# Cross-attention with an image-prompt branch: the output projection in fp32r from high and low parts that Pool splits, and three slots of exponentials

## The chip, the cores and the metric

The kernel runs on one core of one Trainium2 chip. A core has TensorE (PE; its weight loads are listed as PEld), VectorE (DVE), ScalarE (ACT), GpSimd (POOL) and SyncE (SP), which run side by side and wait for one another through semaphores. The metric is the device time of one execution in microseconds (us); lower is better. Three runs of the kernel before gave a median of 502.31 us, from 501.15 to 502.61.

## The reference

Sixteen batches of 256 queries attend, in 20 heads of 16 channels, to 248 text keys with a plain softmax, and to 8 image keys (4 dummy ones and 4 masked by boxes) with a softmax of their own. The two results are added, projected by `w_out`, and the bias and the input are added. Cut to what matters, everything in fp32:

```python
q = split(x @ w_q);  k = split(text @ w_k);  v = split(text @ w_v)     # x (16,256,320), ctx (16,256,512)
out_text = softmax(q @ k.T / 4) @ v                                    # 20 heads, text = first 248 rows
k_ip, v_ip = split(ip @ w_k_ip), split(ip @ w_v_ip)                    # last 8 rows
out_ip = softmax(q @ k_ip.T / 4 + mask(bbox)) @ v_ip
out = (merge(out_text) + merge(out_ip)) @ w_out + b_out + x            # w_out (320,320)
```

## The kernel before, in words

**Numbers.** The projections of q, k and v are fp32r matmuls (one pass over the columns) of operands that are split in a high part (rounded to fp32r) and a low part (the rest): high times high, high times low, low times high. ACT makes high parts, DVE low ones. The values matmul (exponentials times v) and the output projection are plain fp32 matmuls; a plain fp32 matmul stands in the trace as two records.

**Stages.** Batches are made in groups of two. A group has 10 projection tiles (3 of k, 4 of v, 3 of q), numbered n = 10 g + j. The first 12 run alone at the start. The others are hosted, one at a time, in the attention of earlier batches: `batch(t)` attends batch t and hosts 5 tiles of a later group, for t = -1 to 11. The batches t = 12 to 15 host nothing, and `batch(16)` only ends batch 15. Projected q, k and v go to DRAM and come back, stacked anew, for each batch.

**One batch.** Each engine runs its own list, written out by hand: ten slots p = 0 to 9, one for each pair of heads. In slot p PE makes the transposed scores of pair p of batch t (`key_scores`, line 880), and the scores of pair p of batch t + 1 (`query_scores`, line 819), from which DVE takes row maxima (`maxima`, line 664). ACT exponentiates (line 576) into `probs`, four slots of 1024 columns. In even slots PE multiplies by v, four heads (a quad) at a time (`values`, line 895); odd slots host a tile. The tables at the end of the file say in which slot the rest stands. For each of the 5 quads: ACT copies the result from PSUM (`evacuate`, line 568), DVE transposes it in 32x32 blocks and takes reciprocals of the sums (`invert`, lines 715 and 718), POOL multiplies and adds the two branches into `o_norm_t` (lines 478 and 483). DVE turns that back, two quads a piece, as c = 0, 1, 2 (`turn_back`, line 723, slots 8, then 2 and 4 of the next batch), and PE projects (`project_out(b, tile of 128 queries, c)`, line 904): tile 0 in slots 3 (c = 0, 1) and 5 (c = 2), tile 1 in slot 9. DVE adds the residual (`finish`, line 733).

**POOL's list.** For each batch b, `normalise(b)` begins with the residual: it waits for the load of x of this batch (`xr_loaded`) and adds the bias (line 468); only then come the quads k = 0 to 4 of batch b. In k = 2 it also spreads the values of the next batch (line 457). POOL, like every engine, works its list strictly in order.

**SP's list.** SP issues nearly all transfers, in order. In `batch(t)` the load of the residual of batch t (line 338) stands behind the store of the last tile of the batch before, a load of context or x, the k stacks and values of later batches, and the store of an output.

**The start.** PE begins `batch(0)` with a wait on the semaphore `small`, which both the load of the output weights (line 302) and that of the bias (line 303) raise; SP issues them behind the row maxima of batch 0 (line 283). x of the second group is loaded between the k stores and the k loads of the first, and split by ACT (line 502) and DVE (lines 628 and 630) between the lone tiles.

Of the kernel before, what the change touches and what calls it, by code (L numbers as in the profile page):

```python
# [4 lines left out]
B, S, D, C = 16, 256, 320, 512  # L5
# [30 lines left out]
def xattn(nc, x, xT, ctxT, ctx_sp, bbox, wq, wk, wv, wk_ip, wv_ip, wo, bias, grid, kaux, vones, out):  # L36
# [12 lines left out]
    with ctx:  # L49
# [6 lines left out]
        probs = sb("probs", [P, 4, 4 * S])  # L56
        o_all = sb("o_all", [P, 2 * SLOTS * S + 3 * OC * S])
# [3 lines left out]
        x_all = sb("x_all", [P, 6 * S])  # L61
        out_sb = sb("out_sb", [P, OT, D])
        wo_sb = sb("wo_sb", [P, OC, D])
# [10 lines left out]
        v_stage = sb("v_stage", [P, 2, D])  # L74
# [6 lines left out]
        raw = sb("raw", [P, XC * GT])  # L81
        sp_ctx_hl = stack2[:, 0:2 * CC * P].rearrange("p (s c n) -> p s c n", s=2, c=CC)
# [7 lines left out]
        o_norm = o_all[:, at:at + 2 * OC * S].rearrange("p (u c n) -> p u c n", u=2, c=OC)  # L90
        o_norm_t = o_all[:, at + 2 * OC * S:at + 3 * OC * S].rearrange("p (c j n) -> p c j n", c=OC, n=32)
# [3 lines left out]
        def x_raw(g):  # L95
            cols = o_all[:, 0:XC * GT] if g < 2 else raw[:, :]
            return cols.rearrange("p (c n) -> p c n", c=XC)
        flat_p = probs[:, :, :].rearrange("p a n -> p (a n)")
        wkip_raw, wvip_raw, wk_raw = (
            flat_p[:, i * CC * D:(i + 1) * CC * D].rearrange("p (c n) -> p c n", c=CC) for i in range(3))  # L100
# [5 lines left out]
        first_q = [flat_p[:, at:at + 2 * GT].bitcast(f32r).rearrange("p (s n) -> p s n", s=2)  # L106
                   for at in (2 * CC * D + 2 * D - 128, 0, CC * D)]
        x_res = x_all[:, 0:2 * OT * D].rearrange("p (u t n) -> p u t n", u=2, t=OT)
        parts = x_all[0:B * NIP, :].rearrange("p (k n) -> p k n", k=6)
        grid_sb, inside, box_mask, dummy_mask = parts[:, 0:2, :], parts[:, 2, :], parts[:, 3, :], parts[0:B, 4, :]  # L110
        zeros = parts[0:B, 5, :]
# [36 lines left out]
        ld = {n: sem("loaded_" + n) for n in ("sp", "wkip", "wvip", "wq", "wk", "wv", "small", "boxes")}  # L148
# [34 lines left out]
        o_ready = sem("o_ready")  # L183
        out_ready, out_done, out_stored = sem("out_ready"), sem("out_done"), sem("out_stored")
# [27 lines left out]
        slot = lambda u, p: (PAIRS * u + p) % 4  # L212
# [20 lines left out]
        def _(sp):  # L233
# [112 lines left out]
            load_x(1)  # L346
# [4 lines left out]
            load_stack_q(0)  # L351
            lone(5, 7)
# [7 lines left out]
            def first_batch():  # L360
                for n in range(TILES, 19):
                    store_tile(n)
# [50 lines left out]
        def _(pool):  # L413
# [7 lines left out]
            pool.memset(o_norm_t[:, :, :, :], 0.0).then_inc(preset, 1)  # L421
            pool.wait_ge(ld["boxes"], 48)
            pool.wait_ge(preset, 4)
# [19 lines left out]
            for par in range(2):  # L443
                pool.memset(slots(par, 0)[1], 1.0).then_inc(preset, 1)
                pool.wait_ge(preset, 5 + 3 * par)
# [13 lines left out]
            def store_special(i):  # L459
# [4 lines left out]
                    .then_inc(ksp_stored, 16)  # L464
            def normalise(b):
# [4 lines left out]
                for k in range(QUADS):  # L470
# [4 lines left out]
                    if k == 2 and b + 1 < B:  # L475
# [6 lines left out]
                    half = (k % 2) * DH  # L482
                    pool.tensor_tensor(o_norm_t[:, k // 2, :, half:half + DH], out[:, 0:S // 32, :],  # L483
                                       out[:, S // 32:, :], ALU.add).then_inc(o_added, 1)
            spread_values(0)
            pool.wait_ge(ld["small"], 32)
            for b in range(B):
                normalise(b)
        @block.scalar
        def _(act):  # L490
# [53 lines left out]
            tile(3)  # L544
            split_x(1)
            for n in (4, 5):
                tile(n)
# [16 lines left out]
            def evacuate(b, k):  # L564
                n = QUADS * b + k
                act.wait_ge(pv_ready, n + 1)
                need(act, turned, n + 1 - SLOTS)
# [421 lines left out]
```

## Time and profile before

| | |
|---|---|
| median of 3 runs | 502.31 us (501.15 to 502.61) |
| the profiled execution, its own time | 503.35 us |
| its span, first to last instruction | 501.4 us |
| mean granted TensorE clock | 0.986 |
| PE busy | 463.9 us, 93% |
| DVE busy | 393.7 us, 79% |
| ACT busy | 277.1 us, 55% |
| POOL busy | 154.6 us, 31% |

Busy time is the time in which an engine had an instruction under way; matmuls overlap, so the start-to-start distance of two of them, not the duration of one, is what one costs. Idle time names the engine, or the transfer, whose semaphore ended it. The tenths by slice on the page show PE at 9 from slice 7 to slice 33 of 40, and the granted clock at 9 in all slices but the sixth and seventh, where it is 7.

### The profile page before, as it was taken

The page shows a single profiled execution, that of the slowest core. Times are in us where ns is not written, and L with a number is a line of the kernel's source. Part 1 is how long each engine was busy: PE and PEld are TensorE (multiplying, and loading weights), DVE is VectorE, ACT ScalarE, POOL GpSimd, SP SyncE. Part 2 cuts the span into 40 slices and gives each one's busy share as a digit, 9 for nine tenths or more (in the row PEclk, how much of TensorE's full clock was granted, in tenths as well). Part 3 has the DMA queues.
Part 4 walks back from the last instruction along what each step waited for, and adds up shares of the span by engine and source line. Part 5 has one row for each costly group of instructions (what it writes and reads, how often), then busy time and mean ns, then how long its engine had stood idle before and what let it go on. Part 6 is the DMA issues. An engine that isn't in the chain of part 4 may idle for free.

```text
span 501.4 us, 11027 instructions
## 1 busy us (share of the span) xinstructions
PE 463.9 (93%) x4250; PEld 316.7 (63%) x4250; DVE 393.7 (79%) x711; ACT 277.1 (55%) x357; POOL 154.6 (31%) x248
## 2 busy tenths in 40 slices
PE   2997949999999999999999999999999998889987
PEld 2785726676666766676667766677667764555543
DVE  4855765887969798887979798787978788999933
ACT  4642213655646664655546664656545656666672
POOL 4271001335423142413223142323313141524442
PEclk9999977999999999999999999999999999999999
DMA  8999967648593866937594775948594655483011
GB/s 265 363 321 338 324 178 211 186 109 251 161 345 92 279 200 176 282 105 263 155 320 126 244 233 149 294 111 272 146 311 144 218 178 156 141 265 90 9 57 54
DMA packets 94853, 101.80 MB, mean 203 GB/s; under 512 B 16896, under 2 KB 81040, under 8 KB 94800
## 3 DMA queue, kind: packets, MB, share of 16 engines
q1 hardware_dynamic: 93108, 97.63, 62.5%
q0 software_dynamic: 1408, 3.40, 2.4%
q8 instruction: 34, 0.56, 0.5%
q14 instruction: 19, 0.16, 0.1%
q10 hardware_dynamic: 284, 0.05, 0.1%
HBM read 67.87 MB, written 33.23 MB: 202 GB/s over the span
## 4 chain that ended last, share of the span: by engine, by line
PE 60%; issue 15%; DVE 12%; POOL 7%; DMA 4%; ACT 1%; SPq 0%; POOLq 0%; DVEq 0%; ACTq 0%
PE pv L895 11%; PE pj L904 8%; PE score_t L880 8%; PE score_q L819 6%; DVE max_cols L664 5%; PE score_q L770 4%; PE score_q L765 4%; PE score_q L771 3%; PE score_q L767 3%; PE score_q L766 3%; PE score_q L772 3%; POOL o_turned L478 3%; POOL o_all L483 2%; PE score_q L774 2%; PE score_q L775 2%
## 5 line engine op out<-in xcount | busy, mean ns | idle before, releaser
L576 ACT ACTIVATE probs<-score_t 128x1024 f32<-128x1024 f32 x155 | 158.4, 1022 | 148.3 <-PE score_t L880 147.3
L664 DVE TENSOR_REDUCE max_cols<-score_q 128x4 fp32r<-128x992 f32 x155 | 183.0, 1181 | 67.2 <-PE score_q L819 66.5
L895 PE MATMUL pv<-probs,v_cur 128*32 128x256 f32 x1920 | 120.2, 383 | 2.2 <-ACT probs L576 2.1
L478 POOL TENSOR_TENSOR o_turned<-o_turned,inv_cols 128x256 f32<-128x256 f32 x80 | 54.1, 676 | 157.7 <-DVE inv_cols L718 157.7
L895 PEld LDWEIGHTS pv<-probs,v_cur 128*32 128x32 f32 x1920 | 54.6, 109 | 40.6 <-issue 3.2
L468 POOL TENSOR_TENSOR x_all<-x_all,bias_sb 128x640 f32<-128x640 f32 x16 | 25.0, 1564 | 140.4 <-DMA x_all<-in_x 133.4
L904 PE MATMUL pj<-wo_sb,o_all 128*128 128x320 f32 x186 | 63.2, 460 | 4.0 <-DVE o_all L723 3.9
L715 DVE STREAM_TRANSPOSE o_turned<-o_all 128x512 f32<-128x512 f32 x80 | 55.7, 696 | 11.2 <-ACT o_all L568 11.0
L568 ACT ACTIVATE o_all<-pv 128x512 f32<-128x512 f32 x80 | 47.9, 599 | 27.4 <-PE pv L895 26.7
L880 PE MATMUL score_t<-q_stack,k_stack 64*128 64x256 f32 x420 | 52.5, 328 | 10.8 <-DMA bias_sb<-in_bias 7.3
L880 PEld LDWEIGHTS score_t<-q_stack,k_stack 64*128 64x128 f32 x420 | 31.8, 187 | 44.3 <-issue 31.4
L819 PE MATMUL score_q<-k_stack,q_stack 64*128 64x256 f32 x420 | 44.9, 292 | 2.6 <-DMA q_stack<-q_parts 1.1
L904 PEld LDWEIGHTS pj<-wo_sb,o_all 128*128 128x128 f32 x186 | 31.3, 189 | 19.4 <-DVE o_all L723 6.7
L765 PE MATMUL score_q<-wv_hl,c_hi 128*128 128x320 f32 x116 | 40.3, 347 | 1.0 <-DVE qk_out L644 1.0
L483 POOL TENSOR_TENSOR o_all<-o_turned 128x128 f32<-128x128 f32 x80 | 37.8, 472 | 6.3
L819 PEld LDWEIGHTS score_q<-k_stack,q_stack 64*128 64x128 f32 x420 | 32.6, 187 | 9.3 <-issue 6.6
L767 PE MATMUL score_q<-wv_hl,c_hi 128*128 128x320 f32 x116 | 35.9, 309 | 0.0
L766 PE MATMUL score_q<-wv_hl,c_lo 128*128 128x320 f32 x116 | 35.8, 309 | 0.0
L666 DVE TENSOR_REDUCE max_cols<-score_q 128x4 fp32r<-128x32 f32 x155 | 28.0, 181 | 0.0
L522 ACT ACTIVATE qk_out<-score_q 128x512 fp32r<-128x512 f32 (+1 forms) x40 | 23.5, 587 | 6.5 <-PE score_q L774 3.6
L880 PE MATMUL score_t<-stack 64*128 64x256 f32 x200 | 24.5, 322 | 1.8 <-ACT probs L576 1.8
L880 PEld LDWEIGHTS score_t<-stack 64*128 64x128 f32 x200 | 15.0, 185 | 16.5 <-issue 14.1
(171 smaller groups left out, 675.0 us busy)
## 6 DMA issues: line engine op xcount, KB each, us to landing
k_stack<-k_parts SPq DMA_DIRECT2D x33, 320.0 KB, 5.5
q_stack<-q_parts SPq DMA_DIRECT2D x33, 320.0 KB, 5.7
q_parts<-qk_out SPq DMA_DIRECT2D x28, 256.0 KB, 2.8
raw<-in_ctxT SPq DMA_DIRECT2D x13, 512.0 KB, 4.9
k_parts<-qk_out SPq DMA_DIRECT2D x24, 248.0 KB, 5.4
v_stage<-v_rows SPq DMA_DIRECT2D x16, 320.0 KB, 6.3
x_all<-in_x SPq DMA_DIRECT2D x16, 320.0 KB, 6.0
stack<-k_parts SPq DMA_DIRECT2D x15, 320.0 KB, 5.4
```

The lines of the kernel that those rows point to most:

```text
L478: pool.tensor_tensor(out, out, inv_cols[:, n % SLOTS, :].unsqueeze(2).broadcast_to([P, 2 * S // 32, DH]), ALU.mult).then_inc(scaled, 1)
L568: nc.scalar.activation(o_raw[:, n % SLOTS, :], pv[:, :], ACT.Copy).then_inc(o_evac, 1)
L576: nc.scalar.activation(probs[:, slot(t % 2, p), :], key_bank(t, p), ACT.Exp, scale=SCALE)\
L664: nc.vector.tensor_reduce(out=max_cols[:, h, :, at:at + 4:2].rearrange("p t e -> p e t"), in_=both[:, :, :, 0:TEXT], op=ALU.max, axis=AX.X ...
L715: nc.vector.transpose(turned_blocks(n), o_raw[:, n % SLOTS, :].rearrange("p (j n) -> p j n", n=32))\
L765: mm(out, w_hi, x_hi_, start=start, stop=False)
L766: mm(out, w_lo, x_hi_, start=False, stop=False)
L767: return mm(out, w_hi, x_lo_, start=False, stop=stop)
L819: last = mm(score_bank(b, p, e)[:, tile * KEYS:(tile + 1) * KEYS], q_cols(b % 3, p, e, tile * P, P), k_cols(b % 3, p, e, 0, KEYS), start=T ...
L880: last = mm(both[:, 512 * e + S * tile:512 * e + S * tile + S], k_cols(b % 3, p, e, tile * P, P), q_cols(b % 3, p, e, 0, S), start=True, s ...
L895: last = mm(pv[32 * t:32 * t + 32, at:at + S], values_of(u, kind, 4 * k + t), probs[:, slot(u, 2 * k + t // 2), a:a + S], start=kind != 1, ...
L904: last = mm(out_bank(b, t), o_norm[:, b % 2, c, t * P:t * P + P], wo_sb[:, c, :], start=c == 0, stop=c == OC - 1)
```

## The change

It concerns the output projection.

- **PE**: line 904's plain fp32 matmul becomes three fp32r ones for c = 0 and 1 (high x high weight, high x low weight, low x high weight) and two for c = 2. There only one quad is left, of 64 rows: its high and its low part lie side by side (`o_mix`), the weights hold these rows twice, and two matmuls (by high and by low weights) give all four products. `project_out(b, 0, 1)` moves from slot 3 to slot 5. PE waits for `o_split`, which POOL raises, and no longer for DVE's `o_ready`.
- **POOL**: it splits the weights once (`split_wo`); after quads 3 and 4 it splits c = 0 and c = 1 (`split_turned`, a cast and a subtraction of 128x256 each); for the last quad it makes high and low parts ahead of the turn (`mix_last_quad`); and behind quad 0 of the *next* batch it rounds the turned mix (`round_mixed`, a cast of 128x256).
- **Buffers**: three slots of exponentials instead of four; one copy of the turned output instead of two; `wk` is staged elsewhere; the zeros and the padding are made otherwise.
- **Start**: the output weights have a semaphore of their own, they are loaded earlier into `o_all`, and PE waits for their split in `batch(1)`; `batch(0)` doesn't wait for `small` any more. x of the second group is loaded behind the first q stack, and split by ACT and DVE in slots 3 and 4 of `batch(-1)`.

```diff
-        probs = sb("probs", [P, 4, 4 * S])
-        o_all = sb("o_all", [P, 2 * SLOTS * S + 3 * OC * S])
+        probs = sb("probs", [P, 3, 4 * S])
+        o_all = sb("o_all", [P, 2 * SLOTS * S + 5 * S])
+        o_hl = sb("o_hl", [P, 5, S], f32r)
-        wo_sb = sb("wo_sb", [P, OC, D])
+        wo_hl = sb("wo_hl", [P, 2, OC, D], f32r)
...
+            def load_wo():
+                sp.wait_ge(x_tail, 2)
+                sp.dma_start(wo_raw, rows(wo)).then_inc(ld["wo"], 16)
             def load_small():
-                sp.dma_start(wo_sb[:, :, :], rows(wo)).then_inc(ld["small"], 16)
                 sp.dma_start(bias_sb[:, :], bias.broadcast_to([P, D])).then_inc(ld["small"], 16)
...
             lone(0, 3)
-            load_x(1)
             load_stack_k(0)
             sp.wait_ge(aux_stored, 96)
             load_aux(0)
             lone(3, 5)
             load_stack_q(0)
+            load_x(1)
...
+            def split_wo():
+                pool.wait_ge(ld["wo"], 16)
+                pool.tensor_copy(wo_hl[:, 0, :, :], wo_raw).then_inc(wo_high, 1)
+                pool.wait_ge(wo_high, 1)
+                pool.tensor_tensor(wo_hl[:, 1, :, :], wo_raw, wo_hl[:, 0, :, :].bitcast(f32), ALU.subtract)...
+            def mix_last_quad(b, first, second):
+                both = o_norm_t[:, OC - 1, :, :]
+                pool.tensor_tensor(first, first, second, ALU.add).then_inc(mix_step, 1)
+                pool.wait_ge(mix_step, 2 * b + 1)
+                pool.tensor_copy(both[:, :, 0:DH].bitcast(f32r), first).then_inc(mix_step, 1)
+                pool.wait_ge(mix_step, 2 * b + 2)
+                pool.tensor_tensor(both[:, :, DH:2 * DH], first, both[:, :, 0:DH], ALU.subtract)\
+                    .then_inc(o_added, 1)
+            def round_mixed(b):
+                pool.wait_ge(o_ready, OC * (b + 1))
+                pool.tensor_copy(o_mix, o_norm[:, 0, :]).then_inc(o_split, 1)
+            def split_turned(b, c):
+                pool.wait_ge(o_ready, OC * b + c + 1)
+                need(pool, out_ready, OT * b)
+                pool.tensor_copy(o_hi[:, c, :], o_norm[:, c, :]).then_inc(o_high, 1)
+                pool.wait_ge(o_high, 2 * b + c + 1)
+                pool.tensor_tensor(o_lo[:, c, :], o_norm[:, c, :], o_hi[:, c, :].bitcast(f32), ALU.subtract)\
+                    .then_inc(o_split, 1)
...
+                    if k == 0 and b:
+                        round_mixed(b - 1)
+                    if k >= 3:
+                        split_turned(b, k - 3)
...
-                        if p % 2 == 0:
-                            need(act, pv_ready, QUADS * t + (p - 4) // 2 + 1)
+                        need(act, pv_ready, QUADS * t + (p - 3) // 2 + 1)
...
                 dve.wait_ge(o_added, QUADS * b + min(2 * c + 2, QUADS))
-                if c == 0:
-                    need(dve, out_ready, OT * (b - 1))
+                need(dve, o_split, (OC * b, OC * (b - 1) + 2, OC * b + 1)[c])
...
                 if t == 0:
-                    pe.wait_ge(o_ready, OC * b + c + 1)
+                    pe.wait_ge(o_split, OC * b + c + 1)
...
+                if c < OC - 1:
+                    mm(to, o_hi[:, c, cols], w_hi, start=c == 0, stop=False)
+                    mm(to, o_hi[:, c, cols], w_lo, start=False, stop=False)
+                    last = mm(to, o_lo[:, c, cols], w_hi, start=False, stop=False)
+                else:
+                    mm(to, o_mix[:, cols], w_hi, start=False, stop=False)
+                    last = mm(to, o_mix[:, cols], w_lo, start=False, stop=True)
...
             def batch(t):
+                if t == 1:
+                    pe.wait_ge(wo_split, 1)
                 if t == 0:
-                    pe.wait_ge(ld["small"], 32)
...
-OUT = {3: [(0, 0), (0, 1)], 5: [(0, 2)], 9: [(1, 0), (1, 1), (1, 2)]}
+OUT = {3: [(0, 0)], 5: [(0, 1), (0, 2)], 9: [(1, 0), (1, 1), (1, 2)]}
```

On POOL, from the last quad of one batch to the first two quads of the next, the list before reads as follows (`o_turned` holds a quad's transposed result, `x_all` the residual, `o_all` the sums that DVE turns back):

```order
L478 TENSOR_TENSOR o_turned<-o_turned,inv_cols 128x16x16
L483 TENSOR_TENSOR o_all<-o_turned 128x8x16
L468 TENSOR_TENSOR x_all<-x_all,bias_sb 128x640
L478 TENSOR_TENSOR o_turned<-o_turned,inv_cols 128x16x16
L483 TENSOR_TENSOR o_all<-o_turned 128x8x16
```

In the changed kernel the same stretch is this (`o_hl` holds the high and low parts that PE reads, line 502 is the bias on the residual, line 491 the rounding of the mix of the batch before):

```order
L512 TENSOR_TENSOR o_turned<-o_turned,inv_cols 128x16x16
L483 TENSOR_TENSOR o_turned<-o_turned 128x8x16
L485 CAST o_all<-o_turned 128x8x16
L487 TENSOR_TENSOR o_all<-o_turned,o_all 128x8x16
L495 CAST o_hl<-o_all 128x256
L497 TENSOR_TENSOR o_hl<-o_all,o_hl 128x256
L502 TENSOR_TENSOR x_all<-x_all,bias_sb 128x640
L512 TENSOR_TENSOR o_turned<-o_turned,inv_cols 128x16x16
L518 TENSOR_TENSOR o_all<-o_turned 128x8x16
L491 CAST o_hl<-o_all 128x256
```

Five instructions are new here; four stand ahead of the bias on the residual, and the cast of line 491 stands behind it and behind quad 0.

On PE, slot 5 of a batch with hosted tiles reads before (lines 880 and 819 are the two kinds of scores, `pj` the bank of the projection, line 774 the first matmul of the hosted tile):

```order
L880 MATMUL score_t<-q_stack,k_stack 128x256 x4
L819 MATMUL score_q<-stack 128x256 x4
L904 MATMUL pj<-wo_sb,o_all 128x320
L774 MATMUL score_q<-c_hi,wk_hl 128x512
```

and in the changed kernel:

```order
L924 MATMUL score_t<-stack 128x256 x4
L863 MATMUL score_q<-k_stack,q_stack 128x256 x4
L950 MATMUL pj<-wo_hl,o_hl 128x320
L951 MATMUL pj<-wo_hl,o_hl 128x320
L952 MATMUL pj<-wo_hl,o_hl 128x320
L954 MATMUL pj<-wo_hl,o_hl 128x320
L955 MATMUL pj<-wo_hl,o_hl 128x320
L818 MATMUL score_q<-c_hi,wk_hl 128x512
```

The slot now has the three matmuls of c = 1, which stood in slot 3, and the two of c = 2 (lines 954 and 955); the hosted tile stands behind all of them.

## Rows read from the trace of the kernel before

**Rows 1.** Windows: us, busy us of each engine, PE clock, DMA.

```profile
0.00:67.00 67.00, 53.25 (x292) 42.70 (x292) 42.32 (x66) 28.37 (x41) 20.65 (x36) 1.00 0.92 309
67.00:83.00 16.00, 8.04 (x30) 5.83 (x30) 6.67 (x11) 2.14 (x3) 0.00 (x0) 0.57 0.89 244
...
103.00:414.00 311.00, 307.45 (x2883) 210.47 (x2882) 260.48 (x473) 180.60 (x235) 94.23 (x147) 1.00 0.68 208
```

**Rows 2.** Timeline of PE, batch 13, slots 3 and 5: start, us, what.

```profile
441.71 1.34 PE L904 MATMUL pj<-wo_sb,o_all 128*128 128x320 f32 x4
442.98 0.51 PE L819 MATMUL score_q<-stack 64*128 64x256 f32 x4
...
445.75 0.81 PE L904 MATMUL pj<-wo_sb,o_all 128*128 128x320 f32 x2
446.49 0.51 PE L819 MATMUL score_q<-stack 64*128 64x256 f32 x4
```

**Rows 3.** Timeline of PE, a hosted v tile, ten matmuls apart.

```profile
265.98 0.31 PE L766 MATMUL score_q<-wv_hl,c_lo 128*128 128x320 f32 x1
...
267.45 0.31 PE L767 MATMUL score_q<-wv_hl,c_hi 128*128 128x320 f32 x1
```

**Rows 4.** Timeline of all engines, batch 3, slots 3 to 6.

```profile
168.44 1.19 SPq L338 DMA_DIRECT2D x_all<-in_x  x1
...
174.06 0.81 PE L904 MATMUL pj<-wo_sb,o_all 128*128 128x320 f32 x2
...
174.62 1.58 POOL L468 TENSOR_TENSOR x_all<-x_all,bias_sb 128x640 f32<-128x640 f32 x1 [7.54 <-DMA x_all<-in_x]
...
174.93 0.39 PE L771 MATMUL score_q<-x_hi,wq_hl 128*128 128x512 f32 x1
...
175.16 0.40 PE L772 MATMUL score_q<-x_lo,wq_hl 128*128 128x512 f32 x1
```

**Rows 5.** Timeline of POOL, batch 3, behind the bias.

```profile
176.86 0.46 POOL L483 TENSOR_TENSOR o_all<-o_turned 128x128 f32<-128x128 f32 x1
```

**Rows 6.** POOL's line 457, all its instructions: min/median/max ns.

```profile
L457 POOL COPY v_cur<-v_stage x32: 447/454/1324, 57.6 to 469.5; 128x320 f32<-128x320 f32 x32
```

**Rows 7.** Timeline of PE and POOL, slot 5 of batches 1 and 11.

```profile
117.21 0.81 PE L904 MATMUL pj<-wo_sb,o_all 128*128 128x320 f32 x2
117.89 1.58 POOL L468 TENSOR_TENSOR x_all<-x_all,bias_sb 128x640 f32<-128x640 f32 x1 [7.69 <-DMA x_all<-in_x]
...
401.14 1.56 POOL L468 TENSOR_TENSOR x_all<-x_all,bias_sb 128x640 f32<-128x640 f32 x1 [6.97 <-DVE o_all L723]
401.15 0.81 PE L904 MATMUL pj<-wo_sb,o_all 128*128 128x320 f32 x2
```

**Rows 8.** Timeline of POOL and PE, batches 13 and 14.

```profile
449.64 1.54 POOL L468 TENSOR_TENSOR x_all<-x_all,bias_sb 128x640 f32<-128x640 f32 x1 [8.34 <-DMA x_all<-in_x]
...
463.96 1.56 POOL L468 TENSOR_TENSOR x_all<-x_all,bias_sb 128x640 f32<-128x640 f32 x1 [2.67 <-DMA x_all<-in_x]
...
465.74 0.81 PE L904 MATMUL pj<-wo_sb,o_all 128*128 128x320 f32 x2
```

**Rows 9.** Timeline of DVE and PE, start of batch 0.

```profile
68.05 0.18 DVE L666 TENSOR_REDUCE max_cols<-score_t 128x4 fp32r<-128x32 f32 x1
...
69.99 1.23 DVE L624 TENSOR_TENSOR c_lo<-o_all,c_hi 128x1024 fp32r<-128x1024 f32 x1
...
74.21 0.80 PE L880 MATMUL score_t<-q_stack,k_stack 64*128 64x256 f32 x4 [7.31 <-DMA bias_sb<-in_bias]
...
76.89 0.80 PE L819 MATMUL score_q<-k_stack,q_stack 64*128 64x256 f32 x4
```

**Rows 10.** Timeline of PE, the first hosted tile of batch 0, three matmuls apart.

```profile
81.20 0.63 PE L772 MATMUL score_q<-c_lo,wk_hl 128*128 128x512 f32 x1
...
82.48 0.51 PE L772 MATMUL score_q<-c_lo,wk_hl 128*128 128x512 f32 x1
```

**Rows 11.** Timeline of PE, the first tile of the second group.

```profile
39.37 0.47 PE L770 MATMUL pj<-c_hi,wk_hl 128*128 128x512 f32 x1 [2.19 <-DVE c_lo L624]
```

More of the change, by code:

```diff
@@ L97, in x_raw @@
             return cols.rearrange("p (c n) -> p c n", c=XC)
+        flat_wo = wo_hl[:, :, :, :].rearrange("p s c n -> p (s c n)")
+        wo_raw = o_all[:, 0:OC * D].rearrange("p (c n) -> p c n", c=OC)
         flat_p = probs[:, :, :].rearrange("p a n -> p (a n)")
         wkip_raw, wvip_raw, wk_raw = (
-            flat_p[:, i * CC * D:(i + 1) * CC * D].rearrange("p (c n) -> p c n", c=CC) for i in range(3))
+            w[:, at:at + CC * D].rearrange("p (c n) -> p c n", c=CC)
+            for w, at in ((flat_p, 0), (flat_p, CC * D), (staged.rearrange("p a n -> p (a n)"), 0)))
         vsp_out = flat_p[:, 2 * CC * D:2 * CC * D + D]
@@ L147, in xattn @@
         covered = score_q[0:B, 512 + P:512 + P + S]
-        ld = {n: sem("loaded_" + n) for n in ("sp", "wkip", "wvip", "wq", "wk", "wv", "small", "boxes")}
+        ld = {n: sem("loaded_" + n) for n in ("sp", "wkip", "wvip", "wq", "wk", "wv", "small", "wo", "boxes")}
         w_high = sem("w_high")
@@ L211, in turned_blocks @@
             return o_turned[:, k * 2 * S:(k + 1) * 2 * S].rearrange("p (j n) -> p j n", n=32)
-        slot = lambda u, p: (PAIRS * u + p) % 4
+        slot = lambda b, p: (PAIRS * b + p) % 3
         def there(b):
@@ L360, in first_batch @@
             def first_batch():
-                for n in range(TILES, 19):
+                for n in range(TILES, 15):
+                    store_tile(n)
+                load_wo()
+                for n in range(15, 19):
                     store_tile(n)
@@ L481, in normalise @@
                     need(pool, o_ready, OC * (b - 1) + k // 2 + 1)
-                    half = (k % 2) * DH
-                    pool.tensor_tensor(o_norm_t[:, k // 2, :, half:half + DH], out[:, 0:S // 32, :],
-                                       out[:, S // 32:, :], ALU.add).then_inc(o_added, 1)
+                    half, first, second = (k % 2) * DH, out[:, 0:S // 32, :], out[:, S // 32:, :]
+                    if k < QUADS - 1:
+                        pool.tensor_tensor(o_norm_t[:, k // 2, :, half:half + DH], first, second, ALU.add)\
+                            .then_inc(o_added, 1)
+                    else:
+                        mix_last_quad(b, first, second)
+                    if k == 0 and b:
+                        round_mixed(b - 1)
+                    if k >= 3:
+                        split_turned(b, k - 3)
             spread_values(0)
-            pool.wait_ge(ld["small"], 32)
+            split_wo()
+            pool.wait_ge(ld["small"], 16)
             for b in range(B):
                 normalise(b)
+            round_mixed(B - 1)
         @block.scalar
@@ L543, in _ @@
                 tile(n)
-            tile(3)
-            split_x(1)
-            for n in (4, 5):
+            for n in range(3, 6):
                 tile(n)
@@ L573, in batch @@
                         act.wait_ge(st_ready, PAIRS * t + p + 1)
-                        if p % 2 == 0:
-                            need(act, pv_ready, QUADS * t + (p - 4) // 2 + 1)
-                        nc.scalar.activation(probs[:, slot(t % 2, p), :], key_bank(t, p), ACT.Exp, scale=SCALE)\
+                        need(act, pv_ready, QUADS * t + (p - 3) // 2 + 1)
+                        nc.scalar.activation(probs[:, slot(t, p), :], key_bank(t, p), ACT.Exp, scale=SCALE)\
                             .then_inc(exp_done, 1)
@@ L585, in batch @@
                         split_c(g + 1, SPLIT_C_HI[p])
+                    if t == -1 and p == 3:
+                        split_x(1)
                     if t == -1 and p == 6:
@@ L709, in _ @@
                 tile(n)
-            dve.wait_ge(preset, 4)
+            dve.wait_ge(preset, 3)
             def invert(b, k):
@@ L755, in batch @@
                         split_c(g + 1, SPLIT_C_LO[p])
+                    if t == -1 and p == 4:
+                        split_x(1)
                     if hosted(t) and t % 2 == 0 and p == SPLIT_X_LO:
```

45 lines of the change are left out of this document (25 added, 20 removed).

## The prediction

> **What bounds the kernel now.** The windows come first. From 103 to 414 us, where tiles are hosted, PE is busy for 307.45 of 311.00 us at full clock, POOL for 94.23 [rows 1]. So PE sets the pace there, and whatever is added to or taken from its list moves the end; POOL has room on average. An average hides in what order POOL comes to things, though, so the timeline of one batch comes second. In batch 3, PE reaches the projection of slot 5 at 174.06. POOL starts the bias on the residual at 174.62, after 7.54 us of idle time that the landing of x ended [rows 4]. That wait costs nothing now: nobody needs what stands behind it soon. The third view is the start. PE stands for 7.31 us before batch 0, until the bias lands at 74.2 [rows 9], and the clock is at 0.57 of full speed on average from 67 to 83 us [rows 1].
>
> **PE's work.** Between the same neighbours (line 904, then 819) two plain fp32 matmuls take 1.27 us and one takes 0.74 [rows 2], so one costs 0.53. An fp32r matmul of the same shape, 128 rows by 320 columns with a weight load of its own, costs 1.47 / 10 = 0.147 [rows 3]. A batch has six of the first, 3.18 us, and will have 3 x 2 + 3 x 2 + 2 x 2 = 16 of the second, 2.35 us: 0.83 less, 13.3 us over 16 batches if nothing waits. By slot: slot 3 loses 2 x 0.53 and gets 3 x 0.147, 0.62 less; slot 5 loses 0.53 and gets 5 x 0.147; slot 9 loses 1.59 and gets 1.18, 0.41 less. The Trainium skill ("TensorE: Matmul & The Clock Gate", Back-to-back issue gap) gives a full-clock matmul its columns at 2.4 GHz and 2.5 ns, 0.136 here; the row has 0.147 and I keep that, and by the page the kernel would be 256 x 0.011 = 2.8 us faster.
>
> **POOL's list, and the new wait in slot 5.** The projection of c = 2 now waits for `round_mixed` of the batch before. In POOL's list this cast stands behind the bias on the *present* batch's residual, and behind the multiply and add of quad 0. So it can't start before x of the present batch has landed. The load of x is not moved: SP issues it at 168.44 in batch 3 [rows 4], behind the same stores and loads as before, all tied to the start of the batch and not to slot 5. From the start of the bias to the end of quad 0's add there are 177.32 - 174.62 = 2.70 us [rows 4, 5]. The cast of 128x256 is not in the trace. The nearest row is a copy of 128x320 that takes 0.45, and 1.32 once [rows 6]; bounds are 0.36 (0.45 by size) and 1.32, and I take 0.4, since the median is 0.454. With 0.2 for two semaphores, an estimate from gaps of 0.04 to 0.1 between such rows, PE is released 3.3 us after the bias starts: at 177.9 in batch 3. Its two matmuls end 0.29 later. Before, it was through at 174.06 + 0.53. If g is the time from the projection of slot 5 to the bias, a batch loses g + 3.3 + 0.29 - 0.53 = g + 3.06 us in slot 5. What slot 3 saves is worth nothing then, because PE only waits longer. Slot 9 still gives 0.41 back.
>
> g is 0.56 in batch 3 [rows 4] and 0.68 and -0.01 in the first and the last of batches 1 to 11 [rows 7]; over these eleven pairs the mean is 0.86, the largest 1.95. Where PE already waits there for DVE's turn, that wait lies inside the new one, since g counts from its end. So each loses 0.86 + 3.06 - 0.41 = 3.5 us, and the eleven lose 38.6. In batch 13 g is 449.64 - 445.75 = 3.89 [rows 2, 8], in batch 12, by the same pair, 3.4: 6.5 and 6.0 us. In batch 14 the residual comes early, g = -1.78 [rows 8], in 15 about the same: 0.9 and 0.6. Together 14.0. The bounds: if everything ahead of x is 2 us quicker, because PE's waits stretch the batches and leave the queues emptier, 15 x 2 = 30 less; if the cast always takes 1.32, 15 x 0.9 = 14 more.
>
> The Trainium skill ("SBUF — State Buffer", Who interferes with whom) has a rule that speaks against this change: GpSimd shares a port pair with VectorE under an exclusive lock, and whoever comes second stands until the other's instruction is done. The longest copy of 1.32 beside the median of 0.45 [rows 6] fits it, but it is rare. By the rule the cast could be held up in every batch, which is the 14 us above and a time of about 596.
>
> The rest of POOL's new work is hidden. Two more instructions for the last quad and four for the two splits are some 3 us a batch; they stand ahead of the wait for x, where POOL was idle for 7.54 us in batch 3 [rows 4]. The high and low parts of c = 0 and c = 1 are thus there before slots 3 and 5. If that cover were gone, it would cost up to 3 us a batch.
>
> **The clock.** PE will stand idle in slot 5 for about 4 us: in batch 3 it comes to c = 2 at 174.06 - 0.62 + 0.44 = 173.88 and goes on at 177.9; with the mean g it is 4.3, and 7 in batches 12 and 13. In the trace the idle stretch of 7.31 us led to half clock [rows 1, 9], while one of 2.19 us passed at full clock [rows 1, 11]. The new waits lie between the two. I expect them to bring the clock down to 1.2 GHz in nearly every batch. A matmul of 512 columns costs 1.28 / 3 = 0.427 at half clock [rows 10] and 0.23 at full [rows 4]. If about the hosted tile of twelve behind the wait runs at half speed, that is 12 x 0.197 = 2.4 us a batch, 31 us for 13 batches. Bounds: 0, and the first dip's own price: PE was busy for 8.04 us in that window [rows 1], of which half is lost, 4.0 a batch or 52 us in all. I take 31, the tile's.
>
> **Three slots of exponentials, the other buffers.** The exponential of pair p now waits for the values matmul that reads pair p - 3. For odd p this is the matmul that PE issues just ahead of that pair's own scores, so the wait for the scores already covers it; for even p the count is the one before. Zero, or at most 0.05 for a second wait on ACT where PE waits for it. `turn_back` of c = 2 waits for the split of c = 0, done a batch's end earlier. Zero as well.
>
> **The start.** PE no longer waits for the bias. Next is DVE: the last row maxima of batch 0 end at 68.23, so scores can start at 68.4 instead of 74.21. But the second scores of batch 1 (before at 76.89) need DVE's first maxima of that batch, which stand behind the context split of 69.99 + 1.23 and take 1.4: 72.6 [rows 9]. That is 4.3 us earlier. Moving the split of x away from between the lone tiles shortens PE's 2.19 us of idle time [rows 11] by some 1.5, and the q stack is no longer behind x in the queue; DVE gets these two instructions back in slot 4, where it has about that much idle time. The clock still dips, since PE works only 1 of the 6 us up to 72.6. The weights are split by about 68 us and first needed after 73, so the new waits there cost nothing. I take -6 us; bounds -1 (DVE or the loads eat it) and -9 (no dip).
>
> **The end.** Behind the last values POOL has two more instructions of 0.46, then a cast and a subtraction for c = 1 (0.4 and about 0.7) and the rounding (0.4), beside 0.43 of DVE's turn; PE then has less to do, 4 x 0.147 for 2 x 0.53. 0.92 + 1.5 - 0.43 is 2.0, less 0.5, and some semaphores: +2, from +1 to +3.
>
> **The sum.** The profiled execution took 503.35 us: 503.35 + 38.6 + 14.0 + 31 - 6 + 2 = 583. The median of the runs was 1.0 below the profiled one, so the forecast is 582.
>
> **Rivals.**
> 1. *The clock holds.* The waits come, but about 4 us are too short for a dip. For it: 2.19 us passed. Against it: it fell within the idle stretch of the start. 583 - 31 - 1 = 551.
> 2. *The residual comes earlier.* With batches longer by a tenth, loads and stores ahead of x drain sooner, and x lands 2 to 3 us earlier against slot 5. For it: in batches 14 and 15 it does. Against: in batches 1 to 11 SP issues it at a fixed distance from the start of the batch, and behind the same bytes. The waits are then 1.5 to 2 us, and the clock holds: 503.35 + 11 x 1.0 + 11 - 6 + 2 - 1 = 520.
> 3. *POOL's wait doesn't count* (no wait behind x, and the rounding is ready right behind DVE's turn). PE then pays the cast and semaphores, 0.6, in place of its gain in slots 3 and 5: even in each batch, and the start's gain is left: 503 - 6 + 2 - 1 = 498.
> 4. *PE's gain comes in full*, on the other side: the high and low parts are all there when PE comes, and 13.3 us go from its list. It decides from the point where the rounding is done by 173.9 in batch 3; x would have to land 4 us earlier than it does [rows 4]. 503.35 - 13.3 - 6 + 2 - 1 = 485.
> That PE doesn't get cheaper at all is ruled out by rows 3: it is the same shape and type.
>
> **Chances.** Forecast 0.60, clock holds 0.17, residual earlier 0.11, POOL's wait doesn't count 0.06, full gain 0.06. A difference of 0.3%, 1.5 us, is what a measurement of this kernel can tell from none. Rivals 3 and 4 are on the fast side, less 0.02 for an end near zero in rival 3: faster 0.10, same 0.02, slower 0.88. The range takes the forecast with half the bound of the clock's price and the cast's, up to 608, and reaches down past rival 1 with a shorter wait, to 536.
>
> **What would show it.** Right: on PE, idle time of about 4 us in slot 5 of each batch, ended by POOL's line 491; POOL's bias (line 502) still released by the load of x, its wait on line 491 short; projection matmuls 0.147 apart; a granted clock that falls in most batches, a mean near 0.92; batches of 33 to 36 instead of 27 to 30 us; the first scores of batch 0 at 68 or before. Wrong: the wait in slot 5 under 2 us, or ended by another; PE's clock at 1.00 from 103 us on, which leaves rival 1; POOL's bias waiting for DVE or PE instead of x.

## The result, and the profile after

The changed kernel took 578.0 us, the median of 4 runs (577.4 to 578.8), beside 502.5 for the kernel before on the same chip: a ratio of 1.150, 95% interval 1.147 to 1.153. The forecast was 582. The profiled execution took 577.77 us, its span is 576.0 and the mean granted clock 0.920.

The windows come first, as before: window, then busy us (and instructions) of PE, PEld, DVE, ACT and POOL, the granted clock, DMA share and GB/s.

```profile
67.00:83.00 16.00, 12.69 (x82) 9.01 (x84) 10.46 (x17) 5.49 (x7) 1.80 (x1) 0.79 0.82 233
103.00:488.00 385.00, 326.97 (x3000) 227.81 (x2998) 266.54 (x487) 185.82 (x241) 132.67 (x233) 0.91 0.57 176
```

With hosted tiles PE stood idle for 385.00 - 326.97 = 58 us, at a mean clock of 0.91; before, it stood idle for 311.00 - 307.45 = 3.55 us at 1.00 [rows 1]. The waits of the whole span name who ended that idle time (us in total, times, longest):

```profile
POOL x_all L502 <- DMA x_all<-in_x: 99.9, 16, 16.2
PE pj L954 <- POOL o_hl L491: 63.9, 15, 6.4
```

In batch 3 (POOL's timeline, the columns as in [rows 4]) the bias is still released by the load of x, and the cast comes behind quad 0:

```profile
180.86 1.53 POOL L502 TENSOR_TENSOR x_all<-x_all,bias_sb 128x640 f32<-128x640 f32 x1 [6.74 <-DMA x_all<-in_x]
182.34 0.62 POOL L512 TENSOR_TENSOR o_turned<-o_turned,inv_cols 128x256 f32<-128x256 f32 x1
183.04 0.46 POOL L518 TENSOR_TENSOR o_all<-o_turned 128x128 f32<-128x128 f32 x1
183.44 0.40 POOL L491 CAST o_hl<-o_all 128x256 fp32r<-128x256 f32 x1
```

and PE's timeline has the wait, and what stands behind it:

```profile
183.89 0.63 PE L954 MATMUL pj<-wo_hl,o_hl 128*128 128x320 f32 x1 [4.83 <-POOL o_hl L491]
184.32 0.47 PE L955 MATMUL pj<-wo_hl,o_hl 128*128 128x320 f32 x1
184.59 0.63 PE L814 MATMUL score_q<-x_hi,wq_hl 128*128 128x512 f32 x1
185.02 0.63 PE L815 MATMUL score_q<-x_hi,wq_hl 128*128 128x512 f32 x1
```

PE is released 183.89 - 180.86 = 3.03 us after the bias starts, and 3.03 to 3.07 in each of the 15 batches. The matmuls of the hosted tile then start 0.43 us apart, where 0.23 is full speed [rows 4]. Three windows show the granted clock (the third figure from the end) before, around and behind this wait:

```profile
179.10:181.30 2.20, 0.00 (x0) 0.00 (x0) 1.59 (x4) 1.18 (x2) 0.44 (x1) 1.00 1.08 386
181.30:188.10 6.80, 4.21 (x10) 3.01 (x10) 0.00 (x0) 0.00 (x0) 4.28 (x8) 0.50 0.43 136
188.10:198.70 10.60, 10.52 (x103) 6.97 (x102) 9.69 (x17) 7.11 (x9) 1.08 (x2) 1.00 0.47 148
```

PE's idle time at line 954 was 3.15 to 5.65 us in batches 1 to 11 (mean 4.55), 6.4 and 5.2 in 12 and 13, and 1.2 and 1.1 in 14 and 15. The granted clock fell to half in each of batches 1 to 13, for 3.4 or 6.8 us, and in neither 14 nor 15. The batches, from their first scores to those of the next, grew by 5.65 us on average in 1 to 11 (30.6 to 36.6 us where they had been 26.5 to 29.9), by 7.1, 6.7 and 0.7 in 12 to 14: 76.6 us in all. Batch 1 began 5.8 us earlier than in the trace before, and everything from batch 15 on took 30.1 us, not 26.4.

### The profile page after: what moved, and what is told of

Read it like the earlier page. It is cut to its first block, busy times and chain, and to the rows that moved or that the text cites. A ratio compares the mean times of both kernels' runs of the same rounds, so it can differ in the third digit from the quotient of the medians.

```text
span 576.0 us, 11409 instructions
## 1 busy us (share of the span) xinstructions
PE 478.7 (83%) x4314; PEld 335.3 (58%) x4314; DVE 391.9 (68%) x711; ACT 277.3 (48%) x357; POOL 205.9 (36%) x361
## 4 chain that ended last, share of the span: by engine, by line
issue 39%; PE 24%; POOL 23%; DVE 10%; DMA 3%; ACT 0%; POOLq 0%; SPq 0%; DVEq 0%
POOL o_turned L512 6%; DVE max_cols L708 5%; POOL x_all L502 4%; POOL o_all L518 4%; POOL o_hl L497 3%; PE score_q L814 3%; PE score_q L815 3%; PE pv L939 3%; PE score_q L863 2%; PE score_t L924 2%; PE score_q L816 2%; POOL o_hl L495 2%; DMA q_stack<-q_parts 1%; POOL v_cur L468 1%; DMA q_parts<-probs 1%
## 5 line engine op out<-in xcount | busy, mean ns | idle before, releaser
L939 PE MATMUL pv<-probs,v_cur 128*32 128x256 f32 x1920 | 122.6, 389 | 2.3 <-ACT probs L618 2.3
L954 PE MATMUL pj<-wo_hl,o_hl 128*128 128x320 f32 x31 | 13.8, 447 | 63.9 <-POOL o_hl L491 63.9
L758 DVE STREAM_TRANSPOSE o_turned<-o_all 128x512 f32<-128x512 f32 x80 | 55.6, 695 | 12.0 <-ACT o_all L611 11.6
L502 POOL TENSOR_TENSOR x_all<-x_all,bias_sb 128x640 f32<-128x640 f32 x16 | 24.6, 1537 | 99.9 <-DMA x_all<-in_x 99.9
L924 PE MATMUL score_t<-q_stack,k_stack 64*128 64x256 f32 x420 | 53.8, 335 | 5.7 <-ACT probs L618 3.8
L954 PEld LDWEIGHTS pj<-wo_hl,o_hl 128*128 128x128 f32 x31 | 7.1, 227 | 67.9 <-POOL o_hl L491 67.9
L809 PE MATMUL score_q<-wv_hl,c_hi 128*128 128x320 f32 x116 | 37.6, 324 | 1.0 <-DVE qk_out L688 1.0
L811 PE MATMUL score_q<-wv_hl,c_hi 128*128 128x320 f32 x116 | 35.8, 309 | 0.0
L518 POOL TENSOR_TENSOR o_all<-o_turned 128x128 f32<-128x128 f32 x64 | 29.2, 457 | 5.0
L950 PE MATMUL pj<-wo_hl,o_hl 128*128 128x320 f32 x62 | 24.2, 390 | 3.9 <-POOL o_hl L497 3.9
```

The lines of the kernel that those rows point to most:

```text
L502: pool.tensor_tensor(x_res[:, u, :, :], x_res[:, u, :, :], bias_sb[:, :].unsqueeze(1).broadcast_to([P, OT, D]), ALU.add).then_inc(biased, 1)
L518: pool.tensor_tensor(o_norm_t[:, k // 2, :, half:half + DH], first, second, ALU.add)\
L758: nc.vector.transpose(turned_blocks(n), o_raw[:, n % SLOTS, :].rearrange("p (j n) -> p j n", n=32))\
L809: mm(out, w_hi, x_hi_, start=start, stop=False)
L924: last = mm(both[:, 512 * e + S * tile:512 * e + S * tile + S], k_cols(b % 3, p, e, tile * P, P), q_cols(b % 3, p, e, 0, S), start=True, s ...
L939: last = mm(pv[32 * t:32 * t + 32, at:at + S], values_of(u, kind, 4 * k + t), probs[:, slot(b, 2 * k + t // 2), a:a + S], start=kind != 1, ...
```

## The experiments

The theory: PE waits in slot 5 for POOL's rounding, because the rounding stands behind POOL's wait for x; the idle time brings the clock down; all else is small. Rivals: PE's new order or the three slots of exponentials cost something too, the fall of the clock costs little, or POOL and DVE hold each other up.

### Taking the wait from in front of the rounding, in four ways

**The bias behind quad 2** (changed kernel).

```diff
-                pool.wait_ge(xr_loaded[u], 8 * (b - u) + 16)
-                pool.tensor_tensor(x_res[:, u, :, :], x_res[:, u, :, :],
...
+                def add_bias():
+                    pool.wait_ge(xr_loaded[u], 8 * (b - u) + 16)
+                    pool.tensor_tensor(x_res[:, u, :, :], x_res[:, u, :, :],
...
                     if k == 0 and b:
                         round_mixed(b - 1)
+                    if k == 2:
+                        add_bias()
```

> The changed kernel with the bias on the residual (and the wait for the load of x ahead of it) moved on POOL from ahead of quad 0 to behind quad 2; nothing else. Theory (the rounding of the mix stands behind the landing of x): PE's waits on the rounding, 63.9 us in all, shrink to under 0.8 us a batch, the clock stays at full speed from 103 us on, and the time is 486 to 496 us: 503.35, less 13.3 of PE's work and 6 at the start, plus 2 at the end and 15 x 0.2 to 0.6 for the cast and its semaphores. Rival 1 (POOL's added work itself makes the parts late, wherever the bias stands): PE still waits over 3 us a batch, over 555 us. Rival 2 (the three slots or the single copy of the turned output hold the kernel up): the same, over 520 us.

Measured: 496.7 us, just above the range expected; the ratio to the kernel before is 0.990 (0.986 to 0.994). In the even batches with hosted tiles PE starts c = 2 some 9.3 us ahead of the bias, and its waits at this line fall from 63.9 to 2.6 us. But the odd batches lose 0.6 us in slot 0, and batch 1 takes 5.71 there in place of 2.93, with a dip of the clock (a stretch at half clock); that is taken up below.

**The residual loaded first** in SP's list of a batch, POOL's list untouched:

```diff
                     load_rows(t, 1)
+                    need(sp, out_done, OT * (t - 1))
+                    load_residual(t)
                 if hosted(t - 1):
...
-                if t >= 0:
-                    load_residual(t)
```

> The changed kernel with SP's load of the residual of batch t moved up to right behind the row maxima's load at the start of batch(t), with the wait for the output tile that last read the buffer. POOL's list is as in the changed kernel. Theory (the landing of x sets the wait): x lands by 8 to 9 us after the start of the batch in place of 14 to 18, POOL's bias no longer holds up the rounding, PE waits under 1 us a batch, full clock, 488 to 500 us. Rival 1 (POOL's added work itself): over 555 us. Rival 2 (the loads that now stand behind x come late): new waits of PE for stacks or values, 500 to 530 us.

Measured: 493.9, ratio 0.984 (0.980 to 0.988). The bias now starts 8.4 to 10.4 us after the start of a batch in 1 to 11, where it had been 13.6 to 18.3; 4.0 us of waiting are left, 1.5 of them in batch 12, with a dip.

**Both, with the bias behind quad 0 and the rounding** (called the joint repair below):

> The changed kernel with the load of the residual first in SP's list of a batch (as in the version that took 493.9) and the bias moved behind quad 0 and the rounding. Theory: the two repairs take away the same wait, so together they leave PE no wait for the rounding at all, and what the early load left (about 4 us of idle time before c = 2, and a dip of the clock in batch 12) goes: 487 to 492. Rival (the rest above 485 lies with DVE and the finish of the batch, not with the wait for x): 492 to 495, no better than the early load alone.

Measured: 491.2, ratio 0.977 (0.975 to 0.980). The dip in batch 12 is gone, but 2.6 us of waiting are left, not none.

**One line moved**, the rounding at the head of POOL's list for a batch, with the wait for x left behind it:

```diff
+                if b:
+                    round_mixed(b - 1)
                 pool.wait_ge(xr_loaded[u], 8 * (b - u) + 16)
...
-                    if k == 0 and b:
-                        round_mixed(b - 1)
```

> The changed kernel with one line moved: POOL rounds the mix of the batch before at the head of its list for a batch, ahead of the wait for x, in place of behind quad 0. Theory (the wait in slot 5 is POOL's wait for x in front of the rounding): PE's idle time on line 491 falls from 63.9 us to under 5, the clock stays full from batch 1 on, the bias keeps its place and its 99.9 us of waiting, and the time is 488 to 496. Rival (quad 0 of POOL is what the next parts need, and stands behind x still): quads 0 to 2 of POOL are late for DVE's turns, PE waits in slots 3 and 5 for the splits, 500 to 520.

Measured: 492.3, ratio 0.980 (0.977 to 0.982). Of this last one, the waits of PE and of POOL, and the window with hosted tiles:

```profile
PE pj L954 <- POOL o_hl L491: 2.6, 6, 1.0
```

```profile
POOL o_hl L491 <- DVE o_all L765: 57.7, 15, 5.1
POOL x_all L504 <- DMA x_all<-in_x: 37.4, 14, 15.7
```

```profile
103.00:400.00 297.00, 294.46 (x2870) 207.10 (x2869) 254.11 (x460) 177.46 (x231) 130.61 (x220) 1.00 0.70 215
```

POOL was expected to keep its 99.9 us of waiting for x. It waits 37.4, since it now spends 57.7 us ahead of that on DVE's turn, which the rounding needs. But the bias itself starts 16.0 us after the start of a batch on average in 1 to 11, as in the changed kernel, and only it and POOL's later work stand behind x. PE is busy for 294.46 of 297 us at full clock, and 86 us of the 578 are gone by one line. That is the cause, shown. The 2.6 us of waiting that are left lie at the same places in the joint repair, where POOL's bias never waits for x: they are waits for DVE's turn, handed on by POOL.

A further run joined this repair with the early load:

> The version that rounds the mix at the head of POOL's list (492.3 us), with the load of the residual first in SP's list of a batch as well. Theory (with the rounding out of the way, nobody that PE needs soon stands behind the wait for x, so its landing time has stopped to matter): 490 to 493, within 0.4% of the version with either repair. Rival (quads 0 and 1 behind the wait for x still delay DVE's turn now and then, which is what is left above 485): 486 to 489.

Measured: 493.2, ratio 0.981 (0.977 to 0.985). It can't be told from either alone, so no gain from an earlier x is left that these runs could show.

### What the clock cost

The changed kernel with 14 matmuls of 512 columns into the tile's own bank put ahead of slot 5's projection, in batches 1 to 11; they add work that nobody reads.

```diff
+                    if p == 5 and hosted(t) and t > 0:
+                        filler(tile_made(t, p))
```

> The changed kernel, and in slot 5 of batches 1 to 11 PE runs 14 extra matmuls of 512 columns (0.233 us each at full clock, 3.3 us) into the bank of the hosted tile, ahead of the projection, so that it is not idle while it waits for the rounding; their results are overwritten. Theory (of the 75 us, about 28 are the clock that the idle PE loses: in the 11 batches some 24): PE is idle for about 1 us in place of 4.6, the clock stays full in batches 1 to 10 or 11 and dips only in 12 and 13, and the time is 550 to 560 us. Rival (the dips cost little, since other engines or transfers set the pace after the wait): 570 to 578 us. Were the wait not tied to x's landing but to PE's own progress, the filler would add its 3.3 us a batch: 600 us or more.

Measured: 561.8, ratio 1.117 (1.111 to 1.124), above the range expected. In batches 1 to 11 PE starts c = 2 3.05 to 3.14 us behind the bias, and the bias starts 16.0 us after the start of a batch on average, both as without the filler. So the release comes where it did; what changes is that PE works through most of the wait, and that the clock stays full in all eleven batches:

```profile
PE pj L954 <- POOL o_hl L491: 30.7, 14, 7.2
```

```profile
103.00:465.00 362.00, 341.38 (x3154) 242.65 (x3150) 266.73 (x487) 186.04 (x241) 130.18 (x229) 1.00 0.60 186
```

The timed runs gain 16 us. The two traces show that this is a difference of two things. Batches 1 to 11 together take 20.1 us less, some 1.8 each. Batches 12 to 14, which have no filler, take 5.4 us more: in batch 12 PE waits 7.2 us in place of 6.4 and the clock is at half for 13.7 us in place of 6.8, and batch 14 waits 2.2 us and has a dip that it did not have. Why these three got worse isn't shown. Two other ways to size the clock's part:

- By the time at half clock. Behind its waits PE ran at half clock for 48 us in batches 1 to 11 of the changed kernel's trace, 56 with 12 and 13. A matmul of 512 columns costs 0.427 there [rows 10] and 0.23 at full clock [rows 4], so 46% of that time is lost: 22 us in the eleven batches, 26 in all.
- By the repair. The changed kernel against the one-line repair is 578.0 - 492.3 = 85.7 us, of which the waits are 63.9 - 2.6 = 61.3. That leaves 24.

So the clock cost 20 to 22 us in eleven batches and 24 to 26 in thirteen. The expectation had the eleven at 24, which is half of their time at half clock, and did not see the loss in the three batches behind.

### The rest of the change alone

**The start** on the kernel before (own semaphore for the weights, loaded earlier; no wait for the bias in batch 0; x of group 2 stays where it was):

> The kernel before with the start of the change alone: the output weights on a semaphore of their own, loaded behind the fourth v tile's store, PE waits for them in batch(1), and batch(0) does not wait for the bias. The projection stays plain fp32. Theory: PE starts batch 0 at 68 to 69 in place of 74.2 us and is at the second scores of batch 1 about 4 us earlier; 497 to 499 us. Rival (the 6 us come from the later load of x of the second group): no change, 502 us.

Measured: 500.7, ratio 0.994 (0.991 to 0.996), which is 3.1 us less by the ratio and 2.6 by the medians. Both the theory's range and the rival's 502 are missed.

**Three slots of exponentials** on the kernel before:

> The kernel before with three slots of exponentials in place of four, and ACT's waits changed accordingly; nothing else. Theory: the values matmul that frees the slot is issued just ahead of the scores that ACT waits for anyway, so the third slot costs nothing: 501 to 504, and ACT's wait for the values matmul stays below 1 us in all. Rival (part of what the changed kernel lost, and of what keeps the repaired one above 485, are the three slots): 505 to 515, with idle time of ACT ended by PE's values matmul, and PE waiting on its scores for ACT.

Measured: 502.2, ratio 0.998 (0.996 to 1.001): no cost that can be seen.

**c = 1 back in slot 3**, on the one-line repair:

```diff
-OUT = {3: [(0, 0)], 5: [(0, 1), (0, 2)], 9: [(1, 0), (1, 1), (1, 2)]}
+OUT = {3: [(0, 0), (0, 1)], 5: [(0, 2)], 9: [(1, 0), (1, 1), (1, 2)]}
```

> The version that rounds at the head of POOL's list (492.3 us), with the projection of c = 1 back in slot 3, where the kernel before has it. Theory: POOL ends the split of c = 1 about 10.3 us after the start of a batch (190.89 in batch 4, which starts at 180.6), and PE is through with c = 0 in slot 3 about 1.5 us earlier: PE waits 1 to 2 us for line 497 in slot 3 of each of batches 1 to 14, 14 to 28 us more with the full clock, 506 to 520; if waits of that length bring half clock too, up to 540. Rival (the move to slot 5 was needless, since POOL has the parts in time; this is what the prediction says of POOL's other new work, that it is hidden): 491 to 494.

Measured: 513.0, ratio 1.020 (1.016 to 1.024), 20.7 us more than with it in slot 5. PE's timeline in slot 3 of batch 4:

```profile
193.72 0.41 PE L950 MATMUL pj<-wo_hl,o_hl 128*128 128x320 f32 x1 [0.98 <-POOL o_hl L497]
```

In batches 1 to 11 this wait is 0.97 or 0.98 in the even batches and 0.28 in the odd ones, shorter than the 1 to 2 us expected, and the clock stays full through them. A second price wasn't foreseen: slot 5 doesn't get shorter by the three matmuls that left it, since PE now waits there for the rounding (line 491), 0.95 in the even and 0.35 in the odd batches. In batch 12 slot 3 waits 2.35 us, with a dip of the clock. The sum is in the range expected, and the move to slot 5 is a part that the change needs: POOL's split of c = 1 is too late for slot 3.

### Why the late bias gave 4 us less than the others

The same move of the bias on the kernel before:

> The kernel before with the residual's bias (and POOL's wait for the load of x) moved behind quad 2, as in the version of the changed kernel that took 496.7. Theory (the place of the wait matters only because the rounding that PE waits for stands behind it): in the kernel before nothing that is needed soon stands behind the wait, so the time doesn't move: 500 to 504, beside the kernel before in the same runs, and PE's idle time in the batches with hosted tiles stays as it was. Rival (quads 0 and 1 behind the wait for x are late for DVE and PE in any case, new rounding or not): it gets 2 to 6 us faster, 497 to 500.

Measured: 507.5, ratio 1.010 (1.006 to 1.013). Theory and rival both lost: the kernel got neither faster nor kept its time, but was 4.8 us slower. The trace points at what the bias now lies beside. These rows are DVE's line 631, the low part of x, in this kernel (ns, min/median/max; 1180 to 1183 in the kernel before), and DVE and POOL at its second instance:

```profile
L631 DVE TENSOR_TENSOR x_lo<-raw,x_hi x6: 2009/2014/2439, 99.8 to 387.2; 128x1024 fp32r<-128x1024 f32 x6
```

```profile
158.26 1.55 POOL L469 TENSOR_TENSOR x_all<-x_all,bias_sb 128x640 f32<-128x640 f32 x1
```

```profile
158.88 2.01 DVE L631 TENSOR_TENSOR x_lo<-raw,x_hi 128x1024 fp32r<-128x1024 f32 x1
```

DVE starts 0.93 us ahead of the end of POOL's bias and takes 0.83 more than usual, as if it stood until POOL was through and then did nearly its whole 1.18. In batch 1 the two lie 1.35 us together and DVE takes 1.26 more; its maxima are late, PE waits 1.81 us for them, and the clock falls to half for 3.4 us. To test this the bias was moved on, behind quad 3, on the kernel before:

> The kernel before with the bias on the residual behind quad 3 of POOL's list. The version with it behind quad 2 was 4.8 us slower than the kernel before, and in it DVE's split of x (the subtraction into x_lo, 128x1024, which takes 1.18 us otherwise) took 2.44 once and 2.01 five times, each time beside POOL's bias, and ended 1.1 us behind the bias. Theory (a two-operand DVE instruction and POOL's stand in each other's way, and that alone made it slower): behind quad 3 the bias no longer falls beside the split of x, which takes 1.18 again in all six, PE's 1.8 us wait in slot 0 of batch 1 and its half clock go, and the time is that of the kernel before, 501 to 504. Rival (a late bias delays POOL's quads or DVE's finish, and gets dearer the later it is): 506 to 512, with the split of x at 1.18 and other waits on DVE's or PE's side.

and, behind the split of c = 0, on the changed one:

> The changed kernel with the bias on the residual behind quad 3 and the split of c = 0, in place of behind quad 2, where it took 496.7. Theory (of the 4.4 us between that version and the one that rounds first, 492.3, all comes from DVE's split of x beside POOL's bias): 491 to 494, with the split of x at 1.18 in all six, batches 3 to 11 with odd numbers at 26.0 to 26.4 us. Rival (the bias behind quad 3 holds up the split of c = 1, and PE waits for line 497 in slot 5): 496 to 510.

Measured: 502.7, ratio 0.999 (0.997 to 1.000), and 492.8, ratio 0.980 (0.978 to 0.983). In the first, the same row as above (in the second, all six take 1181 to 1184):

```profile
L631 DVE TENSOR_TENSOR x_lo<-raw,x_hi x6: 1180/1181/1184, 99.1 to 382.5; 128x1024 fp32r<-128x1024 f32 x6
```

A bias that comes still later costs nothing, once it doesn't lie beside DVE's subtraction. That the two hold each other up, and that the 4 us come from it, is shown by moving the bias alone.

## Why the prediction was right

By the traces the 74.6 us between the two spans are -5.8 up to batch 1, +76.6 in batches 1 to 14 and +3.7 from batch 15 on; the forecast had 79.6. It had 3 us too much in batches 1 to 11, 3.5 too much in 12 and 13, and 1 too little from batch 15 on.

- **POOL's list, the term of 38.6 + 14.0.** Right in place and size. The release was forecast 3.3 us behind the bias and came at 3.03: the cast took 0.40 as taken, the two semaphores less than 0.2. Idle time at c = 2 was forecast at 4.3 on average, and was 4.55; at 7 in batches 12 and 13, and was 6.4 and 5.2. Batches 1 to 11 were forecast to grow by 3.5 and the clock's 2.4, 5.9 together, and grew by 5.65; 12 and 13, by the same terms, by 8.4 and 8.9, and grew by 7.1 and 6.7. The bias started 16.0 us after the start of a batch on average in 1 to 11, where it had been 15.4. So x didn't come earlier in the longer batches, and the rival "the residual comes earlier" is out; only batches 14 and 15 have it early, as in [rows 8].
- **The clock, 31.** Right in that every wait of 3.15 us or more brought it down. The size is somewhat large: 26 by the time at half clock, 24 by the repair. The step was "about the hosted tile of twelve behind the wait runs at half speed": by the trace it was 4.3 us a batch, ten matmuls. The rival "the clock holds" (551) is out.
- **PE's list, 0.83 a batch.** At full clock the matmuls stand 0.141 to 0.150 apart, most of them 0.145 to 0.147, as in [rows 3]. In the joint repair, where no wait lies over it, slot 3 of the odd batches takes 3.06 for 3.70, slot 5 3.45 for 3.25 and slot 9 3.54 for 3.98: -0.64, +0.20, -0.44, where -0.62, +0.21 and -0.41 were worked out. But the gain is not handed on whole. In slot 1 of the even batches PE comes earlier than DVE's maxima free its bank (its second scores stand 0.50 behind the first ones, not 0.34) and the slot takes 3.90, not 3.66; slot 5 of batch 12 takes 2.91 for 1.72. From batch 1 to 15 the joint repair wins 9.0 of 11.6 us. So the rival "PE's gain comes in full" (485) would not have come true even with no wait for x.
- **The start, -6.** The trace agreed (-5.8), and half of that was luck. Batch 1 begins at 99.2, 101.4, 102.1 and 102.9 in four traces with the start of before, and between 97.0 and 99.9 in nine of ten with the new start (102.3 in the other). By the timed runs the start is worth 3.1 us; the later load of x of the second group was not in them, and its own worth was not measured. One profile was too few to read this start by, and about half the term is all that the runs support.
- **The end, +2.** From batch 15 on, 28.9 us in the joint repair against 26.4: +2.5. In the changed kernel it is 1.2 us more, about the 1.1 us that PE waits in slot 5 of batch 15.
- **Hidden work of POOL.** Right for where the change puts it; the run with c = 1 in slot 3 shows that the cover ends there.
- **The contention, up to 14 more.** The cast of line 491 was held up in no batch: it takes 396 to 398 ns in all 16, and each of POOL's other new lines (casts in 485 and 495, subtractions in 487 and 497) keeps within 22 ns in all its instances. The 1.32 in [rows 6] was the same thing as DVE's 2.01, seen from the other side: POOL's copy and DVE's `c_lo` began 0.2 us apart. It recurs in the changed kernel at quad 3 of five of the odd batches, which falls at the start of the next one (1.47 for 0.62), and in the same way before; POOL has room there:

```profile
199.06 1.47 POOL L512 TENSOR_TENSOR o_turned<-o_turned,inv_cols 128x256 f32<-128x256 f32 x1 [3.67 <-DVE inv_cols L761]
```

```profile
198.89 1.16 DVE L668 TENSOR_TENSOR c_lo<-raw,c_hi 128x1024 fp32r<-128x1024 f32 x1
```

The Trainium skill ("SBUF — State Buffer", SBUF: two separate sides) says that a DVE operation with two SBUF inputs and a GpSimd one that reads SBUF exclude each other for a whole instruction. The rows agree, both ways round. The prediction had weighed such a rule for the cast without asking which of DVE's instructions lie beside it: in 15 of the 16 batches none does, in the other one a transpose, and the 14 us didn't come.

The four repairs at 491 to 493 can't be told apart well; the joint one was lowest, 491.2 us, 2.3% below the kernel before and 15% below the changed one. The one-line repair isn't quite free of the contention: in its trace DVE's `c_lo` takes 1.38 to 1.48 us in place of 1.22 in five of its instances, and four copies and an add of POOL's that lie beside them take 1.28 to 1.45 in place of 0.45.

## What to carry to other kernels

When a result that a busy engine needs goes through another engine's list, look at what that list waits for ahead of it: a wait that has cost nothing so far can become the bound, and moving one line may be the whole repair. Count a stall at more than its length, since the clock may fall with it. And before moving an instruction of POOL, look at what DVE has at its new place, two-operand instructions on SBUF above all.

## What the runs showed of the hardware

- PE's idle time of 3.15 us or more in the steady part of the changed kernel brought half clock each time (13 of 13). Shorter waits did both. At full clock passed 0.98, 1.1 and 1.2 us, 2.25 and 2.30 behind the filler, and 2.19 at the start [rows 11]. A dip came with 1.5 us in batch 12 of the early load, 1.81 in batch 1 of the late bias, 2.18 in batch 14 of the run with the filler, and 2.35 in batch 12 with c = 1 in slot 3. So the length of one wait alone doesn't tell.
- DVE's two-operand subtraction on SBUF beside a POOL instruction: the one that comes second is longer by about the time for which they lie together (DVE 1.18 to 2.01 and 2.44, POOL 0.62 to 1.47 and 0.45 to 1.32). DVE's maxima, which read PSUM, did not get longer beside POOL's work: in the changed kernel 1.175 us on average for the 75 that had POOL beside them, 1.181 for the other 80.
